# Two layers on one core: keys of the chunk attention spread over eight heads, head products in one wave of 64 by 64 tiles

## What is computed

```
H = 16; D = DIM // H; CS = 64; SCALE = D ** (-0.5)
attn = jnp.einsum('bhcqd,bhckd->bhcqk', q, k) * SCALE
mask = jnp.triu(jnp.ones((CS, CS), dtype=bool), k=1)
attn = jnp.where(mask, jnp.float32(-65000.0), attn)
attn = jax.nn.softmax(attn, axis=-1)
out_local = jnp.einsum('bhcqk,bhckd->bhcqd', attn, v)
```

## Time and profile before

| what | value |
|---|---|
| runs (3), median | 643.61 us (642.26 to 643.88) |
| the profiled execution | 642.2 us, span 640.5 us |
| busy | PE 593.0 us (93%), DVE 469.1 (73%), ACT 353.0 (55%), POOL 369.8 (58%) |
| mean granted TensorE clock | 0.991 |
| chunk stage | about 186 to 286 us of the span |

### The profile page before, as it was taken

One profiled execution on the slowest core, in us unless ns is written; L12 is line 12 of the kernel. 1 busy time (PEld: TensorE's weight loads), 2 busy tenths in 40 slices (PEclk: granted clock), 3 DMA queues, 4 the chain that ended last, 5 costly groups with the idle time before them and its releaser, 6 DMA issues.

```text
span 640.5 us, 12614 instructions
## 1 busy us (share of the span) xinstructions
PE 593.0 (93%) x4528; PEld 398.6 (62%) x4529; DVE 469.1 (73%) x1097; ACT 353.0 (55%) x710; POOL 369.8 (58%) x420
## 2 busy tenths in 40 slices
PE   4888899899989899969999999999999999999996
PEld 2566799767655566645555554555555543788885
DVE  5767344449968778898777778777777775788986
ACT  2645455436854555525677776866676656442222
POOL 6607400177548433707888887898788879415220
PEclk9999999999999999988999999999999999999999
DMA  9801122120000000000000000000000000000101
GB/s 285 358 2 47 55 67 66 37 54 10 0 1 3 2 3 2 3 2 1 1 1 1 2 1 2 2 0 1 2 1 1 1 1 1 2 1 2 34 1 34
DMA packets 16617, 17.34 MB, mean 27 GB/s; under 512 B 1712, under 2 KB 15024, under 8 KB 16176
## 3 DMA queue, kind: packets, MB, share of 16 engines
q1 hardware_dynamic: 15536, 14.49, 6.8%
q0 software_dynamic: 1024, 2.10, 1.1%
HBM read 11.34 MB, written 5.24 MB: 26 GB/s over the span
## 4 chain that ended last, share of the span: by engine, by line
PE 71%; DVE 12%; POOL 6%; issue 4%; ACT 4%; DMA 3%; SPq 0%; DVEq 0%; ACTq 0%; POOLq 0%
PE ps L2078 12%; PE ps L2068 10%; PE ps L2058 8%; PE ps L2206 5%; DVE region L1116 3%; PE ps L1881 3%; PE ps L1788 3%; PE ps L1771 3%; PE ps L2196 2%; PE ps L2198 2%; PE ps L2197 2%; POOL slots_in L628 2%; PE ps L1969 2%; DMA region<-slots_in 2%; PE ps L1871 2%
## 5 line engine op out<-in xcount | busy, mean ns | idle before, releaser
L1116 DVE TENSOR_REDUCE region<-ps 128x1 f32<-128x512 f32 x256 | 161.1, 684 | 54.3 <-PE ps L2058 53.8
L1561 ACT ACTIVATE region<-ps 128x512 f32<-128x512 f32 x256 | 138.0, 598 | 54.5 <-PE ps L2068 54.2
L775 POOL TENSOR_TENSOR region<-region 128x512 f32<-128x512 f32 x80 | 107.1, 1342 | 26.2 <-ACT region L1561 23.4
L2068 PE MATMUL ps<-qmr,kr 98*128 98x512 f32 x256 | 112.0, 442 | 1.5 <-ACT region L1561 0.8
L2058 PE MATMUL ps<-kr,qmr 96*128 96x512 f32 x256 | 102.4, 410 | 1.7 <-DVE region L1116 0.9
L2078 PE MATMUL ps<-region 128*32 128x512 f32 x512 | 91.8, 599 | 0.0
L2085 PE MATMUL ps<-region,ones 128*32 128x512 f32 x192 | 91.6, 599 | 0.2 <-DVE region L1132 0.2
L780 POOL TENSOR_TENSOR region<-region 128x512 f32<-128x512 f32 x64 | 81.9, 1279 | 12.2 <-ACT region L1561 8.2
L2068 PEld LDWEIGHTS ps<-qmr,kr 98*128 98x128 f32 x256 | 48.8, 192 | 53.6 <-issue 24.7
L2058 PEld LDWEIGHTS ps<-kr,qmr 96*128 96x128 f32 x256 | 49.4, 194 | 13.8 <-DVE region L1116 7.0
L1665 ACT ACTIVATE region<-ps 128x512 f32<-128x512 f32 x36 | 21.5, 598 | 56.8 <-PE ps L2198 56.8
(11 more groups left out here) (286 smaller groups left out, 1189.9 us busy)
## 6 DMA issues: line engine op xcount, KB each, us to landing
region<-in_w SPq DMA_DIRECT2D x2, 2048.0 KB, 13.0
slots_in<-zeros SPq DMA_DIRECT2D x1, 1536.0 KB, 8.7
region<-slots_in SPq DMA_DIRECT2D x6, 256.0 KB, 2.8
slots_out<-og SPq DMA_DIRECT2D x6, 256.0 KB, 2.4
e<-in_e SPq DMA_DIRECT2D x1, 1152.0 KB, 15.5
x<-in_x SPq DMA_DIRECT2D x4, 256.0 KB, 3.9
out<-y SPq DMA_DIRECT2D x3, 256.0 KB, 2.3
e<-in_e SPq DMA_DIRECT2D x1, 576.0 KB, 16.7
```

Source lines behind the costliest of these rows:

```text
L775: ins = pool.tensor_tensor(o, held(tiles[0]), held(tiles[1]), ALU.add)
L1116: dve.tensor_reduce(mxp[:, u // HM, u % HM:u % HM + 1], bank(b), AX.X, ALU.max).then_inc(mx_read, 1)
L1561: act.activation(pm[:, t // 2, t % 2 * HM * P:(t % 2 + 1) * HM * P], bank(SCORE_BANKS[n % 3]), ACT.Exp, scale=SCM).then_inc(p_whole, 1)
L2068: pe.matmul(bank(SCORE_BANKS[n % 3]), kr[0:M_ROWS, t * P:(t + 1) * P], rows_of(i)[0:M_ROWS, :], start=True, stop=True).then_inc(st_filled, 1)
```

## The change

Eight heads in place of four in one product: `mask8` has 8 columns, and a product takes 64 rows (8 heads' features) and 8 x 64 = 512 columns, in 64x64 tiles as the mask does. 4 products of this form make the whole tile, so `chunk_rest` and its semaphore go. There are twice as many copies of keys (8 instead of 4 per group), shared out: group 0 by ACT (6, from PSUM) and DVE (2, from PSUM, a new step behind the drain of the first values); groups 1 to 3 by POOL (3, 5, 5) and ACT (5, 3, 3). A buffer is twice as large: the even one takes the place of `k4`, the odd one lies in two halves, one of them free memory of the region (formerly `moe`), one `s0`, so that copies for odd groups are issued as two halves of 256 columns, and expand(1) waits for gated(3) (`x1_ready`). The order of steps within a tile changes: the first step of `beside` now comes behind weighing and difference, the others behind turning.

```
-HG = 4
+HB = H1 // 2
+FIRST_ACT = 6
+KEYS_POOL = (0, 3, 5, 5)
...
+        k8_first = region.tensor[:, 6144:8192].rearrange("p (c h s) -> p c h s", c=GC // 2, h=HB)
+        k8_last = s0[:, :, :].rearrange("p t d -> p (t d)").rearrange("p (c h s) -> p c h s", c=GC // 2, h=HB)
...
-                 EARLY + 6: [("v1", 0), ("gate", 3), ("xn1", 1), ("xn1", 2)]}
+                 EARLY + 6: [("v1", 0), ("gate", 3), ("xn1", 1), ("xn1", 2), ("first_keys", 0)]}
...
             if i < NT:
-                chunk_order.append(("chunk_scores", i))
-            chunk_order += more[0:1] if i else []
-            if i < NT:
-                chunk_order.append(("chunk_rest", i))
-            if i < NT:
-                chunk_order.append(("chunk_max", i))
+                chunk_order += [("chunk_scores", i), ("chunk_max", i)]
             if i >= 2:
                 chunk_order.append(("chunk_weigh", i - 2))
-            chunk_order += more[1:2]
+            if i < NT:
+                chunk_order.append(("chunk_difference", i))
             if i == 1:
                 chunk_order.append(("exponents", 0))
-            if i < NT:
-                chunk_order.append(("chunk_difference", i))
-            if i == 0:
-                chunk_order += more
+            chunk_order += more[0:1]
             if 2 <= i <= NT:
                 chunk_order.append(("chunk_out", i - 2))
             if 1 <= i <= NT:
                 chunk_order.append(("chunk_turn", i - 1))
-            chunk_order += more[2:]
+            chunk_order += more[1:]
...
                 pool.wait_ge(f_drained, drained_by["k1", g])
-                if g >= 2:
+                if g == 1:
+                    pool.wait_ge(x1_ready, NG)
+                else:
                     pool.wait_ge(s_done, TG * (g - 1))
-                for h in range(HG):
-                    ins = pool.tensor_scalar(k4[:, g % 2, :, h, :], kraw[:, :].rearrange("p (c s) -> p c s", s=CS), mask4[:, h:h + 1],
-                                             None, ALU.mult)
+                for h in range(KEYS_POOL[g]):
+                    for part, keys in zip(k8_parts[g % 2], halves_of(g)):
+                        ins = pool.tensor_scalar(part[:, :, h, :], keys, mask8[:, h:h + 1], None, ALU.mult)
...
+            def first_keys(_):
+                dve.wait_ge(mask_ready, 1)
+                dve.wait_ge(k4_ready, 1)
+                for h in range(FIRST_ACT, HB):
+                    ins = dve.tensor_scalar(k8_even[:, :, h, :], bank(fill_bank("k1", 0)).rearrange("p (c s) -> p c s", s=CS),
+                                            mask8[:, h:h + 1], None, ALU.mult)
+                ins.then_inc(k4_rest, 1)
...
+                for h in range(KEYS_POOL[g], HB):
+                    for part, keys in zip(k8_parts[g % 2], halves_of(g)):
+                        ins = act.activation(part[:, :, h, :], keys, ACT.Copy, scale=mask8[:, h:h + 1])
+                ins.then_inc(k4_rest, 1)
...
                 pe.wait_ge(k4_ready, g + 1)
+                pe.wait_ge(k4_rest, g + 1)
...
                 for b in range(2):
+                    r = slice(CS * b, CS * (b + 1))
                     for c in range(2):
-                        k = (b + c + wave) % 2
-                        r = slice(32 * (2 * k + b), 32 * (2 * k + b + 1))
-                        ins = pe.matmul(ps[CS * c:CS * (c + 1), 4 + 2 * p + b, n * k:n * (k + 1)],
-                                        q1T[r, P * i + CS * c:P * i + CS * (c + 1)],
-                                        k4[r, g % 2, 2 * (i % TG) + c, :, :].rearrange("p h s -> p (h s)"),
+                        ins = pe.matmul(ps[CS * c:CS * (c + 1), 4 + 2 * p + b, :], q1T[r, P * i + CS * c:P * i + CS * (c + 1)],
+                                        k8_of(g, 2 * (i % TG) + c)[r, :, :].rearrange("p h s -> p (h s)"),
                                         start=False, stop=True, skip_group_check=True)
```

More of the change, by code:

```diff
@@ L227, in bass_recurrent_two_layers @@
         amask = sb("amask", [P, CS])
-        mask4 = sb("mask4", [P, HG])
+        mask8 = sb("mask8", [P, HB])
         ident_b = sb("ident_b", [P, P], BF16)
@@ L295, in bass_recurrent_two_layers @@
         vz = region.take(2, 4 * GC, VZ)
-        k4 = region.take(2, GC, HG, CS)
+        k8_even = region.take(GC, HB, CS)
         xsum = region.take(NC)
@@ L324, in bass_recurrent_two_layers @@
         ehl = sb("ehl", [P, 2 * ES, 2 * D], F32R)
+        k8_first = region.tensor[:, 6144:8192].rearrange("p (c h s) -> p c h s", c=GC // 2, h=HB)
+        k8_last = s0[:, :, :].rearrange("p t d -> p (t d)").rearrange("p (c h s) -> p c h s", c=GC // 2, h=HB)
+        k8_parts = [[k8_even], [k8_first, k8_last]]
+        k8_of = lambda g, c: k8_even[:, c] if g % 2 == 0 else (k8_first if c < GC // 2 else k8_last)[:, c % (GC // 2)]
         eh = [ehl[:, e, :] for e in range(ES)]
@@ L505, in bass_recurrent_two_layers, with halves_of @@
         fill_bank = lambda stage, g: {"turn1": 4, "k1": 5, "q1": 6, "v1": 7}[stage] if g == 0 and stage in ("turn1", "k1", "q1", "v1") else 1
-        slot_of = lambda m: 4 * (m // 2 % 2) + 2 * (m // 4) + m % 2
+        def halves_of(g):
+            keys = kraw[:, :].rearrange("p (c s) -> p c s", s=CS)
+            return [keys] if g % 2 == 0 else [keys[:, 0:GC // 2, :], keys[:, GC // 2:GC, :]]
         rows = lambda r, n: r.unsqueeze(1).broadcast_to([P, n, D])
@@ L650, in _ @@
                                              base=0, pattern=[[-1, CS]], channel_multiplier=1))
-            for g in range(D // 32):
-                m_ = mask4[32 * g:32 * (g + 1), :]
+            for g in range(2):
+                m_ = mask8[CS * g:CS * (g + 1), :]
                 link(pool.affine_select(out=m_, in_=m_, compare_op=ALU.is_ge, fill=0.0,
-                                        base=0, pattern=[[-D1, HG]], channel_multiplier=1))
+                                        base=0, pattern=[[-D1, HB]], channel_multiplier=1))
                 link(pool.affine_select(out=m_, in_=m_, compare_op=ALU.is_ge, fill=0.0,
-                                             base=D1 - 1, pattern=[[D1, HG]], channel_multiplier=-1))
+                                             base=D1 - 1, pattern=[[D1, HB]], channel_multiplier=-1))
             link.mark(pool.tensor_copy(amask_b[:, :], amask[:, :]))
@@ L1060, in values1 @@
                        bank(fill_bank("v1", g))[CS:P, :].rearrange("p (n e d) -> p n e d", e=2, d=D1)).then_inc(f_drained, 1)
-            steps = dict(scores=row_max, values=attention_out, added=experts_added, inputs=gate_inputs, gated=gated, turn1=turned1, q1=queries1, v1=values1)
+            steps = dict(scores=row_max, values=attention_out, added=experts_added, inputs=gate_inputs, gated=gated, turn1=turned1, q1=queries1, v1=values1,
+                         first_keys=first_keys)
             for stage, i in late_order:
@@ L1469, in first_keys, with expand_keys @@
                 for h in heads:
-                    ins = act.activation(k4[:, 0, :, h, :], bank(fill_bank("k1", 0)).rearrange("p (c s) -> p c s", s=CS), ACT.Copy,
-                                         scale=mask4[:, h:h + 1])
-                if h == HG - 1:
+                    ins = act.activation(k8_even[:, :, h, :], bank(fill_bank("k1", 0)).rearrange("p (c s) -> p c s", s=CS), ACT.Copy,
+                                         scale=mask8[:, h:h + 1])
+                if h == FIRST_ACT - 1:
                     ins.then_inc(k4_ready, 1)
+            def expand_keys(g):
+                act.wait_ge(f_drained, drained_by["k1", g])
+                if g == 1:
+                    act.wait_ge(x1_ready, NG)
+                else:
+                    act.wait_ge(s_done, TG * (g - 1))
+                for h in range(KEYS_POOL[g], HB):
+                    for part, keys in zip(k8_parts[g % 2], halves_of(g)):
+                        ins = act.activation(part[:, :, h, :], keys, ACT.Copy, scale=mask8[:, h:h + 1])
+                ins.then_inc(k4_rest, 1)
             def keys1(g):
@@ L1501, in late_value @@
                 turned(i, (12,))
-                first_keys((2, 3))
+                first_keys(range(2, FIRST_ACT))
             steps = dict(scores=score, values=late_value, gate=gate, v1=values1,
@@ L1583, in _ @@
             act.wait_ge(s_w1, 80)
-            steps = dict(k1=keys1, v1=values1, qkv=projected1, cross=cross, query=first_queries,
+            steps = dict(k1=keys1, v1=values1, expand=expand_keys, qkv=projected1, cross=cross, query=first_queries,
                          xn1=lambda g: normalise(3, g, x, xn, xn_ready),
@@ L2002, in chunk_weigh @@
                                       vz[:, g % 2, 4 * (2 * (i % TG) + c) + j, 2 * D1 * e:2 * D1 * (e + 2)],
-                                      p1T[:, slot_of(2 * j + e), CS * c:CS * (c + 1)], start=(e == 0), stop=(e == 1),
+                                      p1T[:, 2 * j + e, CS * c:CS * (c + 1)], start=(e == 0), stop=(e == 1),
```

26 lines of the change are left out of this document (10 added, 16 removed).

## The result

| | before | changed |
|---|---|---|
| median of the runs made side by side (4 each) | 642.93 us (640.34 to 643.88) | 652.44 us (649.39 to 653.89) |
| profiled execution, span, mean clock | 642.2, 640.5, 0.991 | 653.14, 651.3, 0.973 |

The ratio is 1.0137, 95% interval 1.0111 to 1.0163: the change makes the kernel about 9 us slower. The four runs of the changed kernel differ more than those of before: spans 647.4, 649.8, 651.3 and 651.9 at mean clocks of 0.989, 0.986, 0.973 and 0.973.

What follows compares the result with a forecast made beforehand. It took tiles 0 to 3 as paced by a DVE, POOL and PE relay, tiles 4 to 15 as PE-bound; 5.7 + 1.6 - 0.2 = +7.1 us gave a median of 650.7, range 646 to 656.

Steps and rivals of the forecast that it cites:

- main case: Whole kernel: late tile 4 plus longer tiles 4 to 15, +7.1 us, 650.7 us in all; chance 46%.
- rival (a): Clock falls to half behind PE's new gap at 186 to 190, adding 1.1 to 3.1: 651.8 to 653.8; 35%.
- Mask and products 1.30: PE's mask (0.29) and new products (1.01) per tile take 1.30 us instead of 1.52, a gain of 0.22.
- Tile 0 at 190.2, gap 4.3, released by DVE: Stage start: tile 0's scores wait for DVE's two key copies, 4.3 us late, with PE idle.
- New x at 200.4: Downstream of tile 0's late start, the new x is ready at 200.4 instead of 198.43, 2.0 late.
- The wait of the new buffer: expand(1) waits for gated(3); POOL's copies run 200.5 to 205.4, so turn1(3) ends at 209.9, 5.3 us late.
- Tile 4 at 214.5: Tile 4's scores start at 214.5 instead of 208.76, 5.7 us late; the first term of the sum.
- Tiles 4 to 15, +1.6: Eleven pitches: PE saves 2.4, drain waits add 3.8, tile 6 adds 1.2, k1(2)'s wait saves 1.0; net +1.6 us.
- The pitches from tile 8 to 15: Sign against the forecast: it is wrong if these pitches fall below the old 5.2 us on average.
- Rival (b), PE alone counts: Only PE's saving of 16 x 0.22 = 3.5 us counts, delays vanish: faster, 640.1 us; 8%.

Runs made afterwards that it cites:

- e10: The changed kernel with every tile's mask product issued twice; ratio 1.0178 to the kernel before.
- e2: The changed kernel with gated(3)'s scale and rows put ahead of expand(1) on POOL; 651.61 us, ratio 1.0130.
- e4: The changed kernel plus four useless 128x512 products on PE while it waits for the first keys; 651.39 us, ratio 1.0123.
- e1: The changed kernel with all eight first key copies on ACT, none on DVE; 646.64 us, ratio 1.0068.
- e7: e6 with, from tile 5, the first fill ahead of the scores and the second behind weighing, before DVE's difference; ratio 1.0002.
- e8: e7 with group 1's keys spread and signalled in two parts and one head moved from ACT to POOL; ratio 0.9952.
- e5: The kernel before with two of its four first key copies moved from ACT to DVE, behind the drain of the first values; ratio 1.0083.
- e9: The kernel before with one wait added: POOL's spreading of group 1 waits for the new x; ratio 1.0111.
- e11: The kernel before with the change's order of steps alone, old products, buffers and copies; ratio 1.0137.
- e6: e1 with group 1's values drained ahead of tile 2's maximum and the spreading of group 1 issued later; ratio 1.0077.
- e12: The kernel of e8 run again on a third chip; 660.27 us against 663.66, ratio 0.9945.

## Why the prediction was right

It said 650.7 (646 to 656), slower with 0.86; it is 652.44. What happened is its main case together with rival (a), the falling clock. Nearly every step that it named is there, but several sizes were off and made up for each other, so that the number came this near is in part luck. By its steps:

- **Mask and products 1.30.** Measured 1.20 (0.34 + 0.86), a gain of 0.32 per tile and not 0.22. I had added 0.17 us for entering the wave, the excess of an old wave over its streaming, and let the mask become cheaper. It is the other way round. The products take 0.86, twice the 0.42 of the earlier trace rows and 0.02, and the mask its old 0.34. e10 separates them: a second mask costs 0.22 to 0.23, so 0.11 of the first belongs, by this reading, to the passage from the 128x128 work ahead of it, which is still there. The Trainium skill, "TensorEngine Tiling (Array Packing)", section "Key Properties", says that a change of tiling mode drains TensorE; these rows agree with it, if the change is the one from the 128x128 work to the mask, and none is left between mask and products. They do not show the drain itself.
- **Tile 0 at 190.2, gap 4.3, released by DVE.** 190.00 and 4.34. New x at 200.4: 200.6.
- **The wait of the new buffer.** The halves on POOL took 0.90 from start to start, not 0.82, and ended at 206.2, not 205.4. turn1(3) ended at 210.51 (predicted 209.9), 0.6 late. But the sentence that ACT's halves "hold back only things that are waiting for DVE until 204.8 anyway" was wrong: ACT's halves held turn1(2), and with the half clock behind that wait this path was as long as POOL's (e2). The sum came out because the two were nearly equal, which is luck.
- **Tile 4 at 214.5.** 214.91. Counted from turn1(0) the prediction has 35.5, with the clock full, and the changed kernel 36.2. In e4, where the clock does not fall at tile 0, it is 35.1, and half clock at tile 3 is still in that. So at full clock the steps were priced too dear by 0.4 us or more, and the clock more than made it up.
- **Tiles 4 to 15, +1.6.** Measured +2.4. PE's saving 11 x 0.32 = 3.5 instead of 2.4. Waits: 0.7 each before qkv(6), cross(0) and cross(2) (predicted 0.85), 0.8 before cum(0) (0.88), none before qkv(7) (0.34), so 3.0 for 3.8; tile 6's weighing 1.85 more (1.2); k1(2)'s wait gone as said (-0.8). These give +0.5. Then the half-clock stretch behind the 3.2 us wait: tile 6 took 9.5 us where it took 8.1 in e1, which has the same wait and no half-clock stretch: 1.5. That makes +2.0; 0.4 stays unassigned. The pitches from tile 8 to 15 were 5.4 us on average, not below the old 5.2.
- **Rival (a).** Its place was right, but its price (1.1 to 3.1) was for the new gap at 186 to 190 alone. The clock fell at that gap (1.2 at tile 4 by e4), again at the gaps of 2.46 and 3.2 us, and in the next part. That last loss, 2.7 us, is no part of the stage: from the turning of the maxima to the first product of the last experts (L2211, before L2196) the changed kernel needs 264.6 us and the kernel before 261.8, with two stretches of half clock at 543.8 and 550.6 us.
- **Rival (b), PE alone counts.** False: 3.5 us of saving are there and overrun by waits. Its condition, that the delays vanish, is what e7 and e8 work towards: in e7 they weigh as much as the saving (1.0002), and in e8 the result turns to faster.

The three costs do not add up. At tile 4 the late start alone is worth 5.5 (e5), the wait of the buffer 6.3 (e9), the order 2.8 (e11, with the adjacent waves in it), 14.6 together; the change with all three is 6.4 late. By my reading each makes idle time in which the others' work fits. The prediction's sum, which replays every engine's queue, had 5.7 there and so came closer than a sum of separate costs would have.

What stays open: why the clock stays full in e1 at gaps of the same length (2.46 and 3.2 us) as those at which it fell in the changed kernel, and why the pair of half-clock stretches at 544 to 554 us comes in some runs. It came in the profiled executions of the changed kernel, e2, e5 and e6, and in each of these the clock had also been half for 10.2 us at the turning of the maxima, against 6.8 in the others. No run varied that by itself. The gain of e8 was not measured on the first chip, and no run parts its two edits.

## What to carry to other kernels

A cheaper operation can lose where its neighbours were moved for its sake: price the new order on the old operations (in e11 it lost as much as the whole change), and each engine's queue behind a new wait, not only that of the engine which waits first. When a fix of one path gains nothing, look for a second of equal length before giving the cause up. Copies that are needed in part should be signalled in parts: half the keys for the first two tiles, with one head moved to POOL, was worth 2.7 us at tile 4 in e8 and 2.2 in e12.

## What the runs showed of the hardware

- At idle gaps of PE of 2.46, 3.20, 4.34 (changed kernel), 4.34 (e5) and 4.56 us (e9) the granted clock fell to 0.50 (1.2 GHz), for 3.4, 3.4, 6.8, 10.2 and 6.8 us; products at 206.33 took 1.92 us instead of 1.03. Filling the gap of 4.3 with four useless products, so that 0.7 of it was left, kept the clock at 1.00 (e4). The length of the gap does not decide alone: e1 has gaps of 2.46 and 3.2 us at the same steps and a full clock, and it has half clock (3.4 us) at a gap of 1.49 us behind tile 15, where the changed kernel waits 1.48 us and keeps the full clock. The Trainium skill, "TensorE: Matmul & The Clock Gate", section "HAM oscillation — how this bites in real kernels", describes idle gaps between bursts and the next burst at the low clock; the changed kernel agrees, and e1 at its gaps of 2.46 and 3.2 us does not.
- Two waves of old products (32x64 tiles, 256 columns) took 1.18 us with a fill between them (before) and 1.34 directly behind each other (e11). A second mask directly behind the first took 0.22 us, the first, behind 128x128 work, 0.34 (e10).
- A key copy of 128x256 took 0.93 us on POOL (0.90 from start to start) and 0.49 on ACT (0.40 from start to start). ACT is more than twice as fast at it, and POOL's half (0.90) is 0.57 of its whole copy of 1.57.
- The same kernel's spans differed by 4.5 us (647.4 to 651.9) with the mean clock (0.989 to 0.973).
